# Six rescales per pass issued as two halves with a signal each, and a re-woven order of segments

## Chip, cores, metric

One Trainium2 chip, one core of it. The metric is device time in microseconds of one execution; lower is better. The whole program, from the first load to the last store, is one launch.

## What is computed

`x` is (64, 64, 128) float32: 64 sequences of 64 tokens with 128 features. Twelve layers follow each other, each on a layer norm of `x` and added to it:

```python
x = x + _L0_xattn_ref(ctx_1024, _layernorm(x), ...)   # 16 heads of attention over context and latents
x = x + _L0_attn_ref(_layernorm(x), ...)              # gated recurrence over the 64 tokens
x = x + _L0_ffn_ref(_layernorm(x), ...)               # 8 LoRA experts, top 2 of 10
x = x + _L1_xattn_ref(_layernorm(x), ctx_1024, ...)   # one-head cross attention
x = x + _L1_attn_ref(_layernorm(x), ...)              # causal linear attention
x = x + _L1_ffn_ref(_layernorm(x), ...)               # a block of its own: attention, then 4 gated experts
x = x + _L2_xattn_ref(ctx_1024, _layernorm(x), ...)   # 8 heads over context and latents
x = x + _L2_attn_ref(_layernorm(x), ...)              # local attention
x = x + _L2_ffn_ref(_layernorm(x), ...)               # 8 experts, top 1 with capacity
x = x + _L3_xattn_ref(_layernorm(x), ctx_1024, ...)   # x W1 plus the mean of the context times W2
x = x + _L3_attn_ref(_layernorm(x), ...)              # convolution and a small state-space scan
x = x + _L3_ffn_ref(_layernorm(x), ...)               # 8 experts, top 1
```

## The kernel before

The 64 sequences go through in 4 passes (`PASSES`) of two *slots*, each slot 8 sequences, which is 512 tokens: four tiles of 128 tokens on the partitions, so a slot's `x` is 128x512 in SBUF. Each slot has its own buffers (`X`, `Z`, `P`, `T`, `big`, `small`, four PSUM banks) and walks through all twelve layers; the two slots share the engines, so that one computes while the other waits.

**Order.** For every engine the program of a slot is a Python generator that yields between *segments*: a segment is a wait or two and the few instructions behind it. `weave(program, ORDER[engine])` steps the two generators by a written-out row of bits, one bit for a segment: 0 takes the next segment of slot 0, 1 that of slot 1. Within a slot the order of segments is fixed; the bits alone say how the two slots are shuffled on that engine. Engines run their instructions strictly in this order: a segment that has to wait holds up whatever is behind it, of the other slot too.

**A norm.** DVE makes the moments of the four tiles (`moments`, L1360 and L1365) and the variance (L1380, signal `var`); POOL takes it to the power -1/2 (`inverse_root`, L1855, signal `rstd`); DVE multiplies the slot's 128x512 by it (`rescale`, L1375, signal `tok`); PE transposes the four tiles into PSUM (`turn`, L457, signal `zT_ps`); ACT copies them out to `Z` (L1089, signal `zT`); then PE starts the layer's matmuls. Where the layer's weights are centred beforehand, the mean isn't subtracted, and `rescale` reads `x` straight from `X`. Six norms of a pass are such, are turned by PE as four tiles, and are touched by the change: `rnn` (the recurrence), `x1` (L1 cross attention), `lin` (linear attention), `loc` (local attention), `ssm`, `m3` (the last experts). The rescales of the others (`m1`, `rms`, `x2`, `x0`, `ctx0`, `ctx1`) stay whole. Six norms in four passes of two slots make 48 rescales.

**Around it.** In the attention over context and latents (`heads`) PE makes scores (L485), DVE their maxima (L1392), ACT the exponentials (L1114), DVE the reciprocal of the sums (L1400), POOL the normalisation (L1882), PE the transposes (L496), the mixing (L576 to L584) and the output projection (`out_of`, L504, 8 matmuls to a tile). The gated experts (`moe1`) run L815 and L825 on PE, L1679 on DVE, L1972 on POOL, L472 on PE. The experts of `moe2` and `moe3` run L868 and L872 (up), L1287 on ACT, L472 (down) on PE. For the first `heads` of the next pass POOL multiplies and shifts the context tokens, 128x1024 each (`affine`, L1892 and L1896); in POOL's program of a slot these two stand right behind the inverse root of `m3`.

```python
def inverse_root(s, i, name, n=4):
    yield
    pool.wait_ge(*on("var", s, i, name))
    pool.tensor_tensor(rstd(s, name, n), variance(s, name, n), mhalf[:, 0:n], ALU.pow)...
...
yield from inverse_root(s, i, "m3")
if i < PASSES - 1:
    yield from kv_context(s, i)
```

## Time and profile before

| | |
|---|---|
| median of 3 runs | 2494.84 us (2493.54 to 2503.49) |
| profiled execution, its own time | 2495.97 us |
| its span in the trace | 2494.2 us |
| PE busy | 2345.5 us, 94% |
| DVE, ACT, POOL busy | 1481.6, 1178.3, 930.0 us |
| granted TensorE clock, mean | 0.988 |

A row of a timeline gives the start and the length in us, the engine, the line, the operation, output<-inputs by name (slot numbers left out), the shape, the count, and in brackets how long the engine had sat idle before it and what ended that. On PE a float32 matmul is two records (a row with x16 is 8 of them); a transpose is one. PEld is PE's weight load, which runs beside PE.

### The profile page before, as it was taken

The page shows a single profiled execution, that of the slowest core. Times are in us where ns is not written, and L with a number is a line of the kernel's source. Part 1 is how long each engine was busy: PE and PEld are TensorE (multiplying, and loading weights), DVE is VectorE, ACT ScalarE, POOL GpSimd, SP SyncE. Part 2 cuts the span into 40 slices and gives each one's busy share as a digit, 9 for nine tenths or more (in the row PEclk, how much of TensorE's full clock was granted, in tenths as well). Part 3 has the DMA queues.
Part 4 walks back from the last instruction along what each step waited for, and adds up shares of the span by engine and source line. Part 5 has one row for each costly group of instructions (what it writes and reads, how often), then busy time and mean ns, then how long its engine had stood idle before and what let it go on. Part 6 is the DMA issues. An engine that isn't in the chain of part 4 may idle for free.

```text
span 2494.2 us, 41897 instructions
## 1 busy us (share of the span) xinstructions
PE 2345.5 (94%) x16412; PEld 1563.5 (63%) x16412; DVE 1481.6 (59%) x4040; ACT 1178.3 (47%) x2994; POOL 930.0 (37%) x853
## 2 busy tenths in 40 slices
PE   8999999999999999999999999999999999999998
PEld 5666665656756665666666665566566666656665
DVE  5457566665575667666564567665555555664653
ACT  4554334455444534545554444445454444354543
POOL 5334253533233335434231344443332242544310
PEclk8999999999999999999999999999999999999999
DMA  5000000000000000000000000000000000000000
GB/s 233 1 1 2 1 9 8 11 1 18 1 1 10 1 1 10 9 10 9 10 1 9 1 1 9 1 10 9 14 1 1 5 1 1 1 1 1 2 1 9
DMA packets 6677, 26.57 MB, mean 11 GB/s; under 512 B 848, under 2 KB 848, under 8 KB 5840
## 3 DMA queue, kind: packets, MB, share of 16 engines
q1 hardware_dynamic: 6480, 23.89, 2.6%
q8 instruction: 130, 2.13, 0.3%
q14 instruction: 67, 0.55, 0.1%
HBM read 21.79 MB, written 2.10 MB: 10 GB/s over the span
## 4 chain that ended last, share of the span: by engine, by line
PE 72%; DVE 17%; POOL 4%; ACT 4%; issue 3%; DMA 0%; SPq 0%; DVEq 0%; POOLq 0%; ACTq 0%
PE ps L472 10%; PE ps L485 7%; PE ps L529 6%; PE ps L504 6%; PE ps L868 4%; PE ps L496 3%; PE ps L608 3%; PE ps L457 3%; PE ps L583 3%; PE ps L576 3%; PE ps L630 3%; PE ps L581 2%; PE ps L825 2%; PE ps L815 2%; PE ps L657 2%
## 5 line engine op out<-in xcount | busy, mean ns | idle before, releaser
L1882 POOL TENSOR_TENSOR P<-P,small 128x384 f32<-128x384 f32 x384 | 317.2, 849 | 550.1 <-DVE small L1400 549.8
L1114 ACT ACTIVATE P<-ps,small 128x192 f32<-128x192 f32 x768 | 313.6, 420 | 155.1 <-DVE small L1392 153.5
L1855 POOL TENSOR_TENSOR small<-small,mhalf 128x4 f32<-128x4 f32 x112 | 129.0, 1152 | 547.2 <-DVE small L1380 315.4
L485 PE MATMUL ps<-kvT,big 128*128 128x192 f32 x1536 | 314.1, 335 | 6.7 <-DVE big L1407 2.5
L485 PEld LDWEIGHTS ps<-kvT,big 128*128 128x128 f32 x1536 | 248.6, 191 | 89.7 <-issue 52.8
L1392 DVE TENSOR_REDUCE small<-ps 128x2 f32<-128x384 f32 x384 | 210.1, 551 | 107.5 <-PE ps L485 100.2
L472 PEld LDWEIGHTS ps<-wts,P 128*128 128x128 f32 x1920 | 231.5, 192 | 43.8 <-issue 30.0
L472 PE MATMUL ps<-wts,P 128*128 128x128 f32 x1920 | 249.0, 279 | 5.2 <-POOL P L1972 2.6
L1972 POOL TENSOR_TENSOR P<-T 128x512 f32<-128x512 f32 x96 | 126.6, 1319 | 206.6 <-ACT T L1261 107.7
L504 PEld LDWEIGHTS ps<-value,big 128*128 128x128 f32 x1536 | 177.8, 192 | 25.8 <-issue 19.6
L504 PE MATMUL ps<-value,big 128*128 128x128 f32 x1536 | 188.0, 277 | 0.0
L529 PE MATMUL ps<-kvT,score 128*128 128x512 f32 x384 | 179.5, 609 | 5.9 <-ACT kvT L1089 4.7
L496 PE MATMUL ps<-cst,P 128*128 128x128 f32 x1152 | 166.5, 278 | 18.6 <-POOL P L1882 9.2
L496 PEld LDWEIGHTS ps<-cst,P 128*128 128x128 f32 x1152 | 132.5, 143 | 50.4 <-issue 18.6
L1114 ACT ACTIVATION_READ_ACCUMULATOR P<-ps,small 128x1 f32 x768 | 156.8, 204 | 0.0
L1287 ACT ACTIVATE P<-ps,col 128x512 f32<-128x512 f32 x128 | 81.2, 683 | 132.9 <-PE ps L872 132.8
L372 POOL TENSOR_TENSOR big<-big,cst 128x1024 f32<-128x1024 f32 x48 | 106.6, 2222 | 68.9 <-ACT big L1279 39.3
L1458 DVE SCALAR_TENSOR_TENSOR X<-ps,small,X 128x128 f32<-128x128 f32 x256 | 71.9, 343 | 98.9 <-PE ps L472 93.4
L608 PEld LDWEIGHTS ps<-Vbd,P 128*64 128x64 f32 x3072 | 98.2, 138 | 48.3 <-issue 34.7
L1597 DVE TENSOR_REDUCE small<-ps 128x8 f32<-128x512 f32 x128 | 87.7, 685 | 59.7 <-PE ps L630 59.5
L529 PEld LDWEIGHTS ps<-kvT,score 128*128 128x128 f32 x384 | 69.8, 193 | 83.5 <-issue 73.7
L1131 ACT ACTIVATE big<-ps 128x512 f32<-128x512 f32 x96 | 57.2, 596 | 132.5 <-PE ps L496 132.2
(281 smaller groups left out, 4476.8 us busy)
## 6 DMA issues: line engine op xcount, KB each, us to landing
ctok<-ctok_dram SPq DMA_DIRECT2D x8, 512.0 KB, 3.5
ctxT<-ctx_dram SPq DMA_DIRECT2D x8, 512.0 KB, 3.5
wts<-weights_dram SPq DMA_DIRECT2D x1, 2530.0 KB, 23.9
wts<-weights_dram SPq DMA_DIRECT2D x1, 2189.0 KB, 18.3
X<-x_dram SPq DMA_DIRECT2D x8, 256.0 KB, 3.0
big<-fold_dram SPq DMA_DIRECT2D x2, 1024.0 KB, 9.2
out_dram<-X SPq DMA_DIRECT2D x8, 256.0 KB, 2.0
wts<-weights_dram SPq DMA_DIRECT2D x1, 1536.0 KB, 27.0
```

Source lines behind the costliest of these rows:

```text
L372: return engine.tensor_tensor(big[s][:, 1024 * (t % 2):1024 * (t % 2) + 1024].rearrange("p (b j t) -> p b j t", b=2, t=SEQ), src[:, 128 * ...
L472: m = pe.matmul(part(s, k, t), tile_of(src, t), w, start=first and t == 0 and c == 0, stop=last and t == TILES - 1 and c == len(pairs) - 1)
L485: m = pe.matmul(ps[s][:, at:at + KEYS], big[s][:, BANK * b + 128 * p:BANK * b + 128 * p + 128], kvT[s][:, keys_at(b):keys_at(b) + KEYS], s ...
L496: m = pe.transpose(part(s, k, p), probs(s, j)[:, PAIR * p + at:PAIR * p + at + 128], C("ident"))
L504: m = pe.matmul(part(s, 1, t), big[s][:, 1024 * t + 128 * k:1024 * t + 128 * k + 128], value[:, at:at + 128], start=(t == 0 and k == 0), s ...
L529: m = pe.matmul(bank(s, qp_bank(g, r) + k), score[:, 128 * block_of(h, nh):128 * block_of(h, nh) + 128], latents(s), start=True, stop=True)
L608: m = pe.matmul(ps[s][64 * bb:64 * bb + 64, at:at + 18], src(bb, j), Vbd[s][:, 18 * (8 * b + j):18 * (8 * b + j) + 18], start=True, stop=True)
L1114: m = act.activation(probs(s, b // 2)[:, to:to + KEYS], ps[s][:, at:at + KEYS], ACT.Exp, bias=small[s][:, 4 * e + p:4 * e + p + 1], accum_ ...
L1392: dve.tensor_reduce(small[s][:, at:at + 2], ps[s][:, BANK * k:BANK * k + 2 * KEYS].rearrange("p (c k) -> p c k", k=KEYS), AX.X, ALU.max, n ...
L1855: pool.tensor_tensor(rstd(s, name, n), variance(s, name, n), mhalf[:, 0:n], ALU.pow).then_inc(*sig("rstd", s))
L1882: m = pool.tensor_tensor(view, view, over(small[s][:, at:at + 2], 2, [128, 2, KEYS]), ALU.mult)
L1972: pool.tensor_tensor(P[s][:, 1024 + 512 * (k % 2):1536 + 512 * (k % 2)], tmp(s, k % 2), tmp(s, 2 + k % 2), ALU.mult)\
```

## The change

`rescale_halves` issues the multiplication as two instructions of 128x256, tiles 0 and 1 and then tiles 2 and 3, each with its own signal on `tok`. `turn_halves` waits for the first signal before the transposes of tiles 0 and 1, and for the second before those of tiles 2 and 3; both waits lie in one segment, with no yield between them. The counts of `tok` are lengthened to fit. The bits of four engines are rewritten (each has as many as before, SP's are unchanged); one line of each table stands here.

```diff
 ORDER = dict(
     pe=(2496, int(""
-        "4120180e82000011000000000033dbffdf375f56bac10c1af4ddee629cc55cb06914148810afbdc018a1ca1dd3aea84c3e9c"
+        "20120316012000010800000200013bbfffe375f56bac8860cf4edeec616c55cb039141144409fba01e8a1c61ba9db58463e9"
...
+HALVED = ["rnn", "x1", "lin", "loc", "ssm", "m3"]
...
-MANY = {"kv": KV, "var": VARS, "rstd": VARS, "tok": TOKENS, ...
+MANY = {"kv": KV, "var": VARS, "rstd": VARS, "tok": halves(TOKENS), ...
...
+                def turn_halves(s, i, name, k, src):
+                    for t in range(TILES):
+                        if t % 2 == 0:
+                            pe.wait_ge(*on("tok", s, i, name if t else name + ".0"))
+                        m = pe.transpose(part(s, k, t), tile_of(src, t), C("ident"))
+                    m.then_inc(*sig("zT_ps", s))
...
-                    pe.wait_ge(*on("tok", s, i, "rnn"))
-                    turn(s, 0, N[s])
+                    turn_halves(s, i, "rnn", 0, N[s])          # likewise x1, lin, loc, ssm, m3
...
+                def rescale_halves(s, i, name, dst, src):
+                    yield
+                    dve.wait_ge(*on("rstd", s, i, name))
+                    for h in range(2):
+                        dve.tensor_tensor(by_tile(dst)[:, 2 * h:2 * h + 2, :], by_tile(src)[:, 2 * h:2 * h + 2, :],
+                                          over(rstd(s, name)[:, 2 * h:2 * h + 2], 2, [128, 2, D]), ALU.mult).then_inc(*sig("tok", s))
...
-                        yield from rescale(s, i, name, dst, src)
+                        yield from rescale_halves(s, i, name, dst, src)
```

In the changed kernel the lines have other numbers: L457 is L464 (and L471 where halved), L472 is L486, L485 is L499, L496 is L510, L504 is L518, L576 is L590, L868 and L872 are L878 and L882, L1375 is L1389 where halved, L1855 is L1870, L1882 is L1897, L1892 and L1896 are L1907 and L1911.

Between the two orders 776 of PE's 2229 segments that issue anything stand behind another number of the other slot's segments than before, most of them by one; they lie in 214 places, between which the orders agree.

**Place A, `m3` of slot 1 in the third pass.** PE before (`ps_1`, `P_1` are slot 1's; the L457 is the turn of `m3`, the L504 rows are `out_of` of slot 0):

```order
L583 MATMUL ps_0<-Z_0,T_0 128x512
L584 MATMUL ps_0<-Z_0,T_0 128x512
L504 MATMUL ps_0<-value0,big_0 128x128 x8
L457 MATMUL ps_1<-cst,P_1 128x128 x4
L504 MATMUL ps_0<-value0,big_0 128x128 x8
L683 MATMUL ps_0<-ctxT_0,wts 128x512 x2
```

The same place of PE now:

```order
L597 MATMUL ps_0<-Z_0,T_0 128x512
L598 MATMUL ps_0<-Z_0,T_0 128x512
L518 MATMUL ps_0<-value0,big_0 128x128 x16
L471 MATMUL ps_1<-cst,P_1 128x128 x4
L697 MATMUL ps_0<-ctxT_0,wts 128x512 x2
```

The turn has moved behind the last 8 matmuls of slot 0's `out_of`. POOL at the same place, before (`small_1` is slot 1's inverse root of `m3`, `T_1<-ctok_1` and `T_1<-T_1` are `affine` on its context):

```order
L1882 TENSOR_TENSOR P_0<-P_0,small_0 128x2x192 x16
L1855 TENSOR_TENSOR small_1<-small_1,mhalf 128x4
L1892 TENSOR_TENSOR T_1<-ctok_1,col 128x1024
L1896 TENSOR_TENSOR T_1<-T_1,col 128x1024
L1855 TENSOR_TENSOR small_0<-small_0,mhalf 128x4
```

and now:

```order
L1897 TENSOR_TENSOR P_0<-P_0,small_0 128x2x192 x16
L1870 TENSOR_TENSOR small_1<-small_1,mhalf 128x4
L1870 TENSOR_TENSOR small_0<-small_0,mhalf 128x4
L1907 TENSOR_TENSOR T_1<-ctok_1,col 128x1024
L1911 TENSOR_TENSOR T_1<-T_1,col 128x1024
```

Slot 0's inverse root, that of the next recurrence, now stands between slot 1's inverse root of `m3` and the two long operations on the context.

**Place B, PE in the third pass, slot 1 in `moe2` (L472, L868, L872), slot 0 in its first `heads` (L485, L496).** Before:

```order
L472 MATMUL ps_1<-wts,P_1 128x128 x8
L868 MATMUL ps_1<-A_1,wts 128x512 x2
L872 MATMUL ps_1<-mTb_1,pick_b 128x512 x2
L472 MATMUL ps_1<-wts,P_1 128x128 x8
L868 MATMUL ps_1<-A_1,wts 128x512 x2
L872 MATMUL ps_1<-mTb_1,pick_b 128x512 x2
L472 MATMUL ps_1<-wts,P_1 128x128 x16
L496 MATMUL ps_0<-cst,P_0 128x128 x4
L485 MATMUL ps_0<-kvT_0,big_0 128x192 x2
L496 MATMUL ps_0<-cst,P_0 128x128 x8
```

Now:

```order
L486 MATMUL ps_1<-wts,P_1 128x128 x4
L510 MATMUL ps_0<-cst,P_0 128x128 x4
L499 MATMUL ps_0<-kvT_0,big_0 128x192 x2
L486 MATMUL ps_1<-wts,P_1 128x128 x4
L878 MATMUL ps_1<-A_1,wts 128x512 x2
L882 MATMUL ps_1<-mTb_1,pick_b 128x512 x2
L486 MATMUL ps_1<-wts,P_1 128x128 x4
L510 MATMUL ps_0<-cst,P_0 128x128 x4
L486 MATMUL ps_1<-wts,P_1 128x128 x4
L510 MATMUL ps_0<-cst,P_0 128x128 x4
L878 MATMUL ps_1<-A_1,wts 128x512 x2
L882 MATMUL ps_1<-mTb_1,pick_b 128x512 x2
```

Slot 0's transposes and scores, which stood behind the experts of slot 1, are now spread between them.

**Place C, PE at the end of `moe1` of slot 1 in the last pass.** Before (the L472 x8 are the last two of twelve steps of the gated experts, L457 on `ctok_1` the turn of the context, `ps_0` is `heads` of slot 0):

```order
L825 MATMUL ps_1<-A_1,wts 128x512
L472 MATMUL ps_1<-wts,P_1 128x128 x8
L457 MATMUL ps_1<-cst,ctok_1 128x128 x8
L496 MATMUL ps_0<-cst,P_0 128x128 x4
L504 MATMUL ps_0<-value2,big_0 128x128 x8
L576 MATMUL ps_0<-big_0,T_0 128x512
```

Now:

```order
L836 MATMUL ps_1<-A_1,wts 128x512
L518 MATMUL ps_0<-value2,big_0 128x128 x8
L486 MATMUL ps_1<-wts,P_1 128x128 x8
L464 MATMUL ps_1<-cst,ctok_1 128x128 x8
L590 MATMUL ps_0<-big_0,T_0 128x512
```

Slot 0's 8 matmuls of `out_of` have moved ahead of the last two steps of slot 1's experts, and its four transposes further up.

## Rows read from the trace of the kernel before

**Rows 1.** The profile's page: span, busy time by engine, and the chain by engine.

```profile
span 2494.2 us, 41897 instructions
...
PE 2345.5 (94%) x16412; PEld 1563.5 (63%) x16412; DVE 1481.6 (59%) x4040; ACT 1178.3 (47%) x2994; POOL 930.0 (37%) x853
...
PE 72%; DVE 17%; POOL 4%; ACT 4%; issue 3%; DMA 0%; SPq 0%; DVEq 0%; POOLq 0%; ACTq 0%
```

**Rows 2.** PE's waits by releaser: us in total, times, longest.

```profile
PE ps L457 <- DVE P L1375: 33.0, 42, 2.9
PE ps L496 <- POOL P L1882: 9.2, 14, 2.2
```

**Rows 3.** Timeline, `x1` of slot 1, first pass: first of 25 halved turns that waited.

```profile
310.04 1.02 POOL L1855 TENSOR_TENSOR small<-small,mhalf 128x4 f32<-128x4 f32 x1
...
311.10 0.69 DVE L1375 TENSOR_TENSOR P<-X,small 128x512 f32<-128x512 f32 x1 [0.55 <-POOL small L1855]
...
311.85 0.66 PE L457 MATMUL ps<-cst,P 128*128 128x128 f32 x4 [0.42 <-DVE P L1375]
```

**Rows 4.** Timeline, `m3` of slot 0, last pass: the last of the 25.

```profile
2445.02 0.65 PE L457 MATMUL ps<-cst,P 128*128 128x128 f32 x4 [1.80 <-DVE P L1375]
```

**Rows 5.** DVE groups by form: count, then busy us and mean ns of one.

```profile
L1598 DVE TENSOR_TENSOR P<-ps,small 128x512 f32<-128x512 f32 x128 | 88.5, 691 | 4.4
...
L1360 DVE BATCH_NORM_STATS2 small<-X 128x6 f32<-128x128 f32 x384 | 83.3, 279 | 6.1 <-DMA X<-x_dram 4.0
...
L1587 DVE TENSOR_TENSOR kvT<-ps,small 128x128 f32<-128x128 f32 x96 | 28.0, 291 | 3.3
```

**Rows 6.** PE's transposes at L457: duration in ns, min/median/max.

```profile
L457 PE MATMUL ps<-cst,P x352: 272/273/477, 11.8 to 2464.8; 128*128 128x128 f32 x176
```

**Rows 7.** Rescales at L1375 fed from `X`: duration in ns, min/median/max.

```profile
L1375 DVE TENSOR_TENSOR P<-X,small x48: 679/692/2480, 131.1 to 2462.8; 128x512 f32<-128x512 f32 x48
```

**Rows 8.** Timeline, `lin` of slot 1, first pass: first of 14 long rescales.

```profile
330.38 1.27 POOL L1972 TENSOR_TENSOR P<-T 128x512 f32<-128x512 f32 x1
330.44 1.75 DVE L1375 TENSOR_TENSOR P<-X,small 128x512 f32<-128x512 f32 x1 [0.53 <-POOL small L1855]
331.72 2.33 POOL L1892 TENSOR_TENSOR T<-ctok,col 128x1024 f32<-128x1024 f32 x1
```

**Rows 9.** Timeline around place A, `m3` of slot 1, third pass: last of the 14.

```profile
1930.01 1.01 POOL L1855 TENSOR_TENSOR small<-small,mhalf 128x4 f32<-128x4 f32 x1 [8.13 <-DVE small L1380]
...
1930.39 2.05 PE L504 MATMUL ps<-value,big 128*128 128x128 f32 x16
...
1930.98 2.00 POOL L1892 TENSOR_TENSOR T<-ctok,col 128x1024 f32<-128x1024 f32 x1
1931.05 2.48 DVE L1375 TENSOR_TENSOR P<-X,small 128x512 f32<-128x512 f32 x1 [1.12 <-POOL small L1855]
1933.06 2.32 POOL L1896 TENSOR_TENSOR T<-T,col 128x1024 f32<-128x1024 f32 x1
1933.45 0.68 DVE L1432 COPY big<-ps 128x512 f32<-128x512 f32 x1
...
1933.58 0.66 PE L457 MATMUL ps<-cst,P 128*128 128x128 f32 x4 [1.15 <-DVE P L1375]
```

**Rows 10.** Timeline, two scans back to back on DVE, POOL beside them.

```profile
286.85 2.08 POOL L1972 TENSOR_TENSOR P<-T 128x512 f32<-128x512 f32 x1 [1.48 <-ACT T L1261]
...
288.43 3.71 DVE L1472 TENSOR_TENSOR_SCAN big<-T,big 128x512 f32<-128x512 f32 x2
...
289.45 1.61 POOL L1972 TENSOR_TENSOR P<-T 128x512 f32<-128x512 f32 x1 [0.53 <-ACT T L1261]
```

**Rows 11.** The scans at L1472: duration in ns, min/median/max.

```profile
L1472 DVE TENSOR_TENSOR_SCAN big<-T,big x16: 1190/1225/2215, 149.4 to 2115.2; 128x512 f32<-128x512 f32 x16
```

**Rows 12.** POOL groups by form: count, then busy us and mean ns of one.

```profile
L1882 POOL TENSOR_TENSOR P<-P,small 128x384 f32<-128x384 f32 x384 | 317.2, 849 | 550.1 <-DVE small L1400 549.8
```

**Rows 13.** Timeline: the first of 46 waits whose segments now stand further back.

```profile
22.92 2.41 PE L529 MATMUL ps<-kvT,score 128*128 128x512 f32 x5 [1.10 <-ACT kvT L1089]
```

**Rows 14.** Timeline around place C: the last of the 46.

```profile
2276.20 1.26 POOL L1972 TENSOR_TENSOR P<-T 128x512 f32<-128x512 f32 x1 [1.01 <-ACT T L1261]
...
2277.52 1.16 PE L472 MATMUL ps<-wts,P 128*128 128x128 f32 x8 [1.11 <-POOL P L1972]
```

**Rows 15.** Timeline around place B.

```profile
1233.17 2.06 POOL L1882 TENSOR_TENSOR P<-P,small 128x384 f32<-128x384 f32 x2
...
1246.28 0.87 DVE L1458 SCALAR_TENSOR_TENSOR X<-ps,small,X 128x128 f32<-128x128 f32 x3 [11.73 <-PE ps L472]
```

More of the change, by code:

```diff
@@ new lines @@
+        "d930588ed73eb000018bfb2ffcecffd1dc40001008c56b483bc0930120ffd181f870101383a86d33fd6febfbbc28717efb7e"
+        "9acfc54b5bfff6dbee707114148a04fdef5401c918e6c09d54163eb74d30b4c5ae72000038bfb75ff1affb4f44482672eb78"
+        "8286dcfb7fc181102c86940200004c21bfcff936fd6ebffffb785c77075f56ee5928a5d76703911029140503ef3e901c24c9"
+        "9baea857fff7779f27120aad5400007d5dfd4f15d1b4010069bbbc330a01525fbfff1942d00e20800000056bfd97eef375f5"
+        "ff83141ae9bffefeef8ff28cef6b8ca502245053c5eee80b111167de3481cff7fffffb87ffbbdfffff9e292cd1eeb2a22410"
@@ new lines @@
+        "2bec7ff19e1d404e9fffc0f", 16)),
+    act=(1740, int(""
+        "40402207000020008000335fff93f6f4fbbfa7548613430f00901c00083079ecbe87de270440ed9d6218fee366fff6840049"
+        "0de383bc09469e1801a0079e0ccfbdfedbfffde96e60cf3ff5dd4b1b00902c2020cace60ef07de3ca18433b100f2fecb0fff"
+        "f5870cdfaf8823b1dc00c8f9a0010000f4f393fdeffffb3fefedf3102c5aa28f00841048208195db4f63fff73d38401eb489"
+        "8f8ff885f9100d73f7a610113ab768f9c00000009db9e7dbf3fbfbbfffcf9b60b955d12c10416040801eb3bf501fbffffddf"
+        "fcfffff246863cefd2492b1c2ffa00fff1", 16)),
@@ L97 @@
         "67fd", 16)),
     pool=(610, int(""
-        "673400df30532b53182161b93a2fbb7378c7904c253ac34fc0ff53185609d43957dee378c7cb219c0e0dee3a2b53142131b5"
-        "3af57f8db607c0b9807706bc935fa660ac0ae49ffff3be7d1d", 16)),
+        "ca028adf3036335290a1c27a3937bdc9fd2c90489531671fc0ff66225518e8392fbe71f9b58d059a0d0ef635335490a07279"
+        "3cf5df371d23c0b9805c56f4a3cfaa612a0ccc9fffdfe67d1d", 16)),
     sp=(26, int(""
@@ L133, with halves @@
 PROJ = ["rnn.g", "rnn.i", "lin", "lin.v", "m1", "m1.p1", "m1.v", "loc", "loc.v"]
-MANY = {"kv": KV, "var": VARS, "rstd": VARS, "tok": TOKENS, "zT_ps": TURNS, "zT": COPIES, "y_ps": SUMS, "x_biased": BIASED,
+HALVED = ["rnn", "x1", "lin", "loc", "ssm", "m3"]
+def halves(names):
+    return [m for n in names for m in ([n + ".0", n] if n in HALVED else [n])]
+MANY = {"kv": KV, "var": VARS, "rstd": VARS, "tok": halves(TOKENS), "zT_ps": TURNS, "zT": COPIES, "y_ps": SUMS, "x_biased": BIASED,
         "logits": LOGITS, "shifted": LOGITS[:3], "u_exp": LOGITS[:3], "n_proj": PROJ,
@@ L724, in cross @@
                     yield
-                    pe.wait_ge(*on("tok", s, i, "x1"))
-                    turn(s, 0, N[s])
+                    turn_halves(s, i, "x1", 0, N[s])
                     yield
@@ L751, in linear @@
                     yield
-                    pe.wait_ge(*on("tok", s, i, "lin"))
-                    turn(s, 0, N[s])
+                    turn_halves(s, i, "lin", 0, N[s])
                     yield
@@ L847, in local @@
                     yield
-                    pe.wait_ge(*on("tok", s, i, "loc"))
-                    turn(s, 0, N[s])
+                    turn_halves(s, i, "loc", 0, N[s])
                     yield
@@ L947, in ssm @@
                     yield
-                    pe.wait_ge(*on("tok", s, i, "ssm"))
-                    turn(s, 0, N[s])
+                    turn_halves(s, i, "ssm", 0, N[s])
                     for ks in ((0,), (1,), (2, 3)):
@@ L974, in moe3 @@
                     yield
-                    pe.wait_ge(*on("tok", s, i, "m3"))
-                    turn(s, 0, N[s])
+                    turn_halves(s, i, "m3", 0, N[s])
                     yield
@@ L1701, in local @@
                        .then_inc(*sig("x3_sum", s))
-                    yield from rescale(s, i, "loc", N[s], res(s, i))
+                    yield from rescale_halves(s, i, "loc", N[s], res(s, i))
                     yield
```

21 lines of the change are left out of this document (5 added, 16 removed).

## The prediction, made before the changed kernel had run

> **What bounds the kernel now.** I read the page first: PE is busy for 2345.5 of 2494.2 us, no other engine for over 59%, and PE makes 72% of the chain that ended last [rows 1]. So PE is idle for 2494.2 - 2345.5 = 148.7 us in all, and nothing that leaves PE's work as it is can bring more than that; the change takes no matmul away. What the change can move is these 148.7 us. The waits of PE by releaser say what they are made of: the largest group is the turn behind a rescale, 33.0 us in 42 waits, the next is the transposes of `heads` behind POOL, 9.2 us [rows 2]; the rest is spread over some forty small groups. Then I went to the timeline of the six norms. Of their 48 turns 25 waited, the first for 0.42 us [rows 3] and the last for 1.80 us [rows 4], 18.8 us together. The others found their rescale done.
>
> **Part 1, the halves.** An undisturbed rescale takes 0.69 us, and PE's transposes start 0.06 us behind its end (311.10 + 0.69 = 311.79, then 311.85 [rows 3]). The trace has no DVE operation of 128x256 of this kind. A product of 128x128 takes 291 ns and one of 128x512 takes 691 ns [rows 5], so each further column costs 400/384 = 1.04 ns, and 256 columns come to 291 + 133 = 424 ns. Two operations with no wait between them overlap a little: the 384 moments have a mean of 279 ns but cover 83.3 us, 217 ns each [rows 5], so the next starts 62 ns before the end of the last. The second half then starts at 362 ns and ends at 786 ns. The first signal comes 268 ns earlier than now, the last 94 ns later.
>
> On PE four transposes take 0.66 us [rows 3] and one 273 ns [rows 6], so they are 0.13 us apart. Behind the first signal (0.42 + 0.06 = 0.48 us) two transposes issue until 0.74; the second signal is there at 0.79 + 0.06 = 0.85; the last two end at 0.85 + 0.13 + 0.27 = 1.25 us. Now they end at 0.69 + 0.06 + 0.66 = 1.41 us. That is 0.16 us for each turn that waits, 25 x 0.16 = 4 us. The bounds: 25 x 0.27 = 6.7 us, if the second pair were never late, and below nothing the 94 ns that each of 48 rescales adds on DVE, 4.5 us, if DVE were always what PE waits for. DVE is busy for 59% [rows 1] and mostly waits itself, so I take 4 us gained and 0 lost.
>
> **Part 2, POOL and the shared access of a rescale.** The rescales of the six norms lie between 679 and 2480 ns, with a median of 692 [rows 7]; 14 of the 48 took over 0.9 us, the first at 330.44 [rows 8] and the last at 1931.05 [rows 9]. Each long one starts while POOL runs a large operation and ends some 0.5 us after it: POOL's L1892 runs from 1930.98 to 1932.98, the rescale from 1931.05 to 1933.53, and POOL's next, L1896, takes 2.32 us instead of 2.00 [rows 9]. So DVE and POOL hold each other up, a whole instruction at a time. Two scans back to back show what happens between two DVE instructions: each takes 1190 ns alone [rows 11], the pair took 3.71 us, and a POOL operation that came up during the first one (289.45) was through before the second ended [rows 10]. POOL gets in between.
>
> That bears on the halves: where a POOL operation is waiting when the first half ends, the second half waits for all of it. In the order before, the six `m3` of the first three passes have L1892 ahead of the rescale and L1896 right behind, and the second half would wait 2.0 us there [rows 9]. The Trainium skill says the same from the other side (SBUF — State Buffer, section "Who interferes with whom"): a Vector instruction with two inputs in SBUF contends with a GpSimd instruction that reads SBUF, and the one that starts first holds the access for the whole instruction. By it each half asks anew; it speaks against this change wherever POOL has work queued, and the traced scans agree with it.
>
> But POOL's order is changed just there. Place A shows it: the other slot's inverse root now stands between the root of `m3` and L1892. In three of the six (slot 0 in the first and third pass, slot 1 in the third) something stands there now, and in the other three work of the other slot (two or four normalisations, or short operations and an inverse root) stands between L1892 and L1896, so that the long L1896 is not waiting when the first half ends. Where L1892 is late, the rescale is free of it and ends up to 2.48 - 0.69 = 1.8 us earlier; PE waited 1.15 us for it at place A [rows 9] and like times at the other two. Bounds: 0 (normalisations of 849 ns each [rows 12] take the place of L1892) to 3 x 1.15 = 3.5 us; I take 2 us. Against it, second halves that meet a normalisation elsewhere: I take 2 of the 14 at 0.85 us, 2 us. The part comes to 0.
>
> **Part 3, the order.** PE changes in 214 places, half of them exchanges of two neighbouring segments. I went through PE's waits of over 0.1 us and looked at where their segments now stand. 46 of them, 30.0 us in all, have more of the other slot's work ahead than before, the first at 22.92 [rows 13] and the last at 2277.52 [rows 14]; by the length of that work 24.3 us of them could be filled. 13 waits, 6.0 us, have less ahead. At place C PE waited 1.11 us for POOL's L1972 [rows 14], and now does 8 matmuls of `out_of` there, 2.05 us a set of the same size [rows 9]; that wait is filled whole. At place A the moved `out_of` needs the copy L1432, which DVE makes behind the rescale, from 1933.45 to 1934.13 [rows 9]: with the old rescale it would not be ready in time, and the move pays only because POOL's order frees the rescale as well. So of two places looked at, one pays by itself and one by its companion. Place B is of another kind: up to 1246.28 DVE had nothing to do for 11.73 us while PE ran the experts of slot 1, although POOL had slot 0's probabilities ready at 1235.23 [rows 15]. Now slot 0's transposes stand between the experts; PE gains nothing there at once, but slot 0's chain of DVE, ACT and POOL gets some microseconds of lead, and the experts that are left cover its later waits.
>
> A segment put forward into a place where its input isn't ready opens a new wait, and the trace of before can't show these; every one of the filled waits also makes its own slot later. The bounds are 24.3 us gained, and 0. I take half, 12 us, as one of the two places pays alone.
>
> **The sum.** 4 + 0 + 12 = 16 us against the profiled execution's own 2495.97 us gives 2480 us; that execution was 1.1 us over the median of the runs, so against 2494.84 the prediction is 2479 us, 0.6% less. About 0.5%, 12.5 us, is what a measurement of this kernel can tell from no change, so the forecast lies just outside of it, at 2482.4.
>
> **The rivals.**
>
> - *The waits only move* (22%). Both slots' chains are as long as before; a filled wait comes back one segment later, since what was put ahead delays the slot that waits. For it: most waits are under 1 us and spread over the whole span, which is how a well-woven order looks. Against it: 46 waits get cover and 13 lose it. Then part 3 gives 0 and the halves 4 us: 2491 us.
> - *The experts as a reserve pay more* (8%). As at place B, more of the latency of `heads` is hidden than the single waits say. Nearly all of the 24.3 us, the 4 and the 3.5: 2463 us.
> - *POOL takes the gap between the halves* (12%), the one that ends slower. Place: the second half of the 14 rescales that met POOL before. Price: 2.0 us at the 6 of `m3` and at the 2 of `lin` with L1892 behind [rows 8], 0.85 us [rows 12] at the other 6, 8 x 2.0 + 6 x 0.85 = 21 us on DVE, and PE waits within a segment, so nothing can pass. It decides if POOL's order brings its readers there as often as before and the order's fills come to less than 21 - 4 - 12.5 = 4.5 us; with none of them it gives 2494.8 + 21 - 4 = 2512 us. The skill's rule named above is this rival's rule. Against it: place A's new POOL order.
> - The forecast holds the remaining 58%, with a range of its own from 2470 to 2487 us.
>
> **The numbers.** The range reaches from 24.3 + 6.7 + 3.5 us below the median, 2460, to the halves' cost on DVE of 4.5 us with no fill, 2499 us. It leaves out nearly all of the slower rival and a part of the third case, under 2 in 10. Faster by over 0.5%: four fifths of the forecast and all of the large case, 0.55. Within 0.5%: the rest of the forecast and the first rival, 0.33. Slower: 0.12.
>
> **What would show it.** The 48 rescales appear as 96 operations of 128x256 with a median near 424 ns; PE's waits behind them in total fall from 18.8 us to about 14 or less. The rescales of `m3` beside L1907 are fewer than five at over 2 us. PE's busy time stays at 2345 us within a few us and its idle time falls to about 133 us. DVE's longest idle near place B is shorter than 11.73 us. I would be wrong if second halves last over 1 us at many places (then POOL is in the gap), if PE's waits by releaser keep their total under other names (then the waits only moved), or if PE's busy time changes by more than 5 us, since then the interleaving itself costs something that I put at nothing.

## The result: 2526.34 us, 1.2% slower than before

The changed kernel took 2526.34 us (median of 4, 2523.93 to 2528.49), beside 2494.79 us of the kernel before: ratio 1.0116, 95% interval 1.0094 to 1.0139. I had predicted 2479 us and a range up to 2499; the time lies 31.5 us over the kernel before and outside of the range. The page of the changed kernel (span, busy time by engine, chain by engine), to be read beside [rows 1]:

```profile
span 2526.4 us, 41947 instructions
...
PE 2362.1 (93%) x16412; PEld 1573.7 (62%) x16412; DVE 1494.2 (59%) x4088; ACT 1165.8 (46%) x2994; POOL 918.4 (36%) x853
...
PE 68%; DVE 18%; ACT 5%; POOL 4%; issue 4%; DMA 0%; SPq 0%; DVEq 0%; POOLq 0%; ACTq 0%
```

The span grew by 32.2 us. PE's busy time grew by 2362.1 - 2345.5 = 16.6 us with the same 16412 matmuls, and its idle time from 148.7 to 2526.4 - 2362.1 = 164.3 us. The chain is now 68% PE instead of 72%. PE's waits by releaser (us in total, times, longest):

```profile
PE ps L471 <- DVE P L1389: 18.9, 23, 1.7
PE ps L510 <- POOL P L1897: 12.4, 19, 2.3
PE ps L464 <- DVE P L1383: 9.4, 13, 2.8
```

The turns that were halved (L471) waited 18.9 us, as much as the same 48 turns did before (18.8 us). The transposes of `heads` behind POOL grew from 9.2 [rows 2] to 12.4 us. The halves are the new group on DVE (duration in ns, min/median/max):

```profile
L1389 DVE TENSOR_TENSOR P<-X,small x96: 394/421/2222, 133.9 to 2495.3; 128x256 f32<-128x256 f32 x96
```

**Place A** after the change, timeline:

```profile
1952.84 1.01 POOL L1870 TENSOR_TENSOR small<-small,mhalf 128x4 f32<-128x4 f32 x1 [3.53 <-DVE small L1395]
1953.88 0.76 DVE L1389 TENSOR_TENSOR P<-X,small 128x256 f32<-128x256 f32 x2 [1.12 <-POOL small L1870]
...
1959.71 0.60 PE L471 MATMUL ps<-cst,P 128*128 128x128 f32 x4
...
1962.21 1.01 POOL L1870 TENSOR_TENSOR small<-small,mhalf 128x4 f32<-128x4 f32 x1 [8.36 <-DVE small L1395]
1963.18 2.00 POOL L1907 TENSOR_TENSOR T<-ctok,col 128x1024 f32<-128x1024 f32 x1
1963.25 4.35 DVE L1389 TENSOR_TENSOR P<-X,small 128x256 f32<-128x256 f32 x2 [1.12 <-POOL small L1870]
1965.26 2.06 POOL L1911 TENSOR_TENSOR T<-T,col 128x1024 f32<-128x1024 f32 x1
1965.51 0.44 PE L471 MATMUL ps<-cst,P 128*128 128x128 f32 x2 [0.87 <-DVE P L1389]
1967.65 0.44 PE L471 MATMUL ps<-cst,P 128*128 128x128 f32 x2 [1.70 <-DVE P L1389]
```

The rescale of `m3` of slot 1 is free, as forecast: two halves in 0.76 us, and its turn found them ready (the wait of 1.15 us of [rows 9] is gone). But what POOL's order put ahead of L1907 is slot 0's inverse root, and behind an inverse root comes a rescale. The two long operations now meet the halves of slot 0's recurrence: 4.35 us, and PE waits 0.87 and 1.70 us. The meeting moved by one norm. Nor are the other `m3` all free: the six pairs of halves of the first three passes take 1.36, 2.96, 2.55, 1.69, 2.01 and 0.76 us in order of time. And two meetings stand as they stood, at `lin` of slot 1 in the first and the third pass (3.63 and 3.62 us), which are those of [rows 8] in halves:

```profile
334.54 3.63 DVE L1389 TENSOR_TENSOR P<-X,small 128x256 f32<-128x256 f32 x2 [0.54 <-POOL small L1870]
335.82 2.06 POOL L1907 TENSOR_TENSOR T<-ctok,col 128x1024 f32<-128x1024 f32 x1
...
338.22 0.69 PE L471 MATMUL ps<-cst,P 128*128 128x128 f32 x2 [1.71 <-DVE P L1389]
```

**Place C** is filled as forecast; slot 0's 16 records of `out_of` run where PE had waited 1.11 us [rows 14], and no row has a wait:

```profile
2305.59 1.02 PE L836 MATMUL ps<-A,wts 128*128 128x512 f32 x2
2306.45 1.95 PE L518 MATMUL ps<-value,big 128*128 128x128 f32 x16
...
2308.24 1.95 PE L486 MATMUL ps<-wts,P 128*128 128x128 f32 x16
```

### The profile page after: what moved, and what is told of

Read it like the earlier page. It is cut to its first block, busy times and chain, and to the rows that moved or that the text cites. A ratio compares the mean times of both kernels' runs of the same rounds, so it can differ in the third digit from the quotient of the medians.

```text
span 2526.4 us, 41947 instructions
## 1 busy us (share of the span) xinstructions
PE 2362.1 (93%) x16412; PEld 1573.7 (62%) x16412; DVE 1494.2 (59%) x4088; ACT 1165.8 (46%) x2994; POOL 918.4 (36%) x853
## 4 chain that ended last, share of the span: by engine, by line
PE 68%; DVE 18%; ACT 5%; POOL 4%; issue 4%; DMA 0%; SPq 0%; DVEq 0%; POOLq 0%; ACTq 0%
PE ps L486 10%; PE ps L499 6%; PE ps L518 6%; PE ps L543 5%; PE ps L878 4%; PE ps L510 3%; PE ps L622 3%; PE ps L597 3%; PE ps L590 2%; PE ps L644 2%; PE ps L595 2%; PE ps L836 2%; PE ps L826 2%; PE ps L464 2%; PE ps L671 2%
## 5 line engine op out<-in xcount | busy, mean ns | idle before, releaser
L1897 POOL TENSOR_TENSOR P<-P,small 128x384 f32<-128x384 f32 x384 | 318.2, 851 | 551.8 <-DVE small L1415 551.7
L1122 ACT ACTIVATE P<-ps,small 128x192 f32<-128x192 f32 x768 | 314.1, 422 | 148.7 <-DVE small L1407 148.1
L1870 POOL TENSOR_TENSOR small<-small,mhalf 128x4 f32<-128x4 f32 x112 | 127.2, 1136 | 594.2 <-DVE small L1395 318.1
L499 PE MATMUL ps<-kvT,big 128*128 128x192 f32 x1536 | 316.3, 335 | 9.6 <-ACT P L1122 3.5
L499 PEld LDWEIGHTS ps<-kvT,big 128*128 128x128 f32 x1536 | 248.2, 191 | 95.8 <-issue 55.1
L486 PEld LDWEIGHTS ps<-wts,P 128*128 128x128 f32 x1920 | 234.9, 195 | 52.7 <-issue 35.1
L486 PE MATMUL ps<-wts,P 128*128 128x128 f32 x1920 | 254.2, 282 | 8.9 <-DVE P L1808 4.4
L518 PEld LDWEIGHTS ps<-value,big 128*128 128x128 f32 x1536 | 178.2, 192 | 28.3 <-issue 18.4
L518 PE MATMUL ps<-value,big 128*128 128x128 f32 x1536 | 188.9, 278 | 2.0 <-ACT P L1122 1.8
L510 PE MATMUL ps<-cst,P 128*128 128x128 f32 x1152 | 167.3, 278 | 20.1 <-POOL P L1897 12.4
L510 PEld LDWEIGHTS ps<-cst,P 128*128 128x128 f32 x1152 | 132.6, 142 | 50.3 <-issue 17.2
L1269 ACT ACTIVATE T<-ps 128x512 f32<-128x512 f32 x96 | 57.3, 596 | 120.4 <-PE ps L836 120.3
```

What stands on the lines that cost most here:

```text
L486: m = pe.matmul(part(s, k, t), tile_of(src, t), w, start=first and t == 0 and c == 0, stop=last and t == TILES - 1 and c == len(pairs) - 1)
L499: m = pe.matmul(ps[s][:, at:at + KEYS], big[s][:, BANK * b + 128 * p:BANK * b + 128 * p + 128], kvT[s][:, keys_at(b):keys_at(b) + KEYS], s ...
L510: m = pe.transpose(part(s, k, p), probs(s, j)[:, PAIR * p + at:PAIR * p + at + 128], C("ident"))
L518: m = pe.matmul(part(s, 1, t), big[s][:, 1024 * t + 128 * k:1024 * t + 128 * k + 128], value[:, at:at + 128], start=(t == 0 and k == 0), s ...
L1122: m = act.activation(probs(s, b // 2)[:, to:to + KEYS], ps[s][:, at:at + KEYS], ACT.Exp, bias=small[s][:, 4 * e + p:4 * e + p + 1], accum_ ...
L1897: m = pool.tensor_tensor(view, view, over(small[s][:, at:at + 2], 2, [128, 2, KEYS]), ALU.mult)
```

## The experiments

Every ratio is to the kernel before, run beside the version on the same chip; its median there was between 2495.28 and 2500.61 us, so I compare ratios, not medians. Its single executions differ with the granted clock, as 2491.06 us at a mean of 0.992 and 2502.57 us at 0.985 beside e1 to e4. "Old order" means the four tables of the kernel before.

| run | median us | ratio | 95% interval |
|---|---|---|---|
| e1 halves, old order | 2512.17 | 1.0053 | 1.0033, 1.0073 |
| e2 whole rescales, new order | 2519.19 | 1.0087 | 1.0062, 1.0112 |
| e3 halves, one wait, old order | 2518.90 | 1.0081 | 1.0055, 1.0107 |
| e4 `rnn` and `loc` halved, old order | 2494.68 | 0.9984 | 0.9971, 0.9997 |
| e5 whole, PE's table new | 2573.77 | 1.0322 | 1.0302, 1.0342 |
| e6 whole, the other tables new | 2607.00 | 1.0449 | 1.0431, 1.0466 |
| e7 halves, old order, POOL waits | 2491.44 | 0.9985 | 0.9968, 1.0003 |
| e8 whole, old order, POOL waits | 2494.33 | 0.9988 | 0.9973, 1.0004 |
| e9 whole, new order, quiet stretches | 2494.69 | 0.9996 | 0.9986, 1.0005 |
| e10 whole, new order, the others | 2522.01 | 1.0102 | 1.0084, 1.0120 |
| e11 the changed kernel, POOL waits | 2531.03 | 1.0147 | 1.0127, 1.0166 |
| e12 e7 and a second wait of POOL | 2494.74 | 0.9994 | 0.9985, 1.0002 |
| e13 whole, new order 510 to 945 us | 2512.00 | 1.0052 | 1.0034, 1.0070 |
| e14 whole, new order 1480 to 2165 us | 2508.58 | 1.0034 | 1.0022, 1.0046 |
| e15 whole, 100 exchanges on PE | 2535.15 | 1.0150 | 1.0133, 1.0167 |
| e16 whole, 54 exchanges on DVE | 2536.49 | 1.0140 | 1.0118, 1.0162 |
| e17 whole, 37 exchanges that delay no one | 2499.63 | 1.0007 | 0.9994, 1.0020 |
| e18 e7 with these 37 | 2492.55 | 0.9981 | 0.9972, 0.9991 |

### Each part alone: e1 to e4

e1 keeps the halves and takes the old order; e2 the reverse; e3 and e4 vary e1.

```diff
 ORDER = dict(
     pe=(2496, int(""
-        "20120316012000010800000200013bbfffe375f56bac8860cf4edeec616c55cb039141144409fba01e8a1c61ba9db58463e9"
+        "4120180e82000011000000000033dbffdf375f56bac10c1af4ddee629cc55cb06914148810afbdc018a1ca1dd3aea84c3e9c"
...
```

> The halves of all six norms, with the four order tables of the kernel before. Theory H (POOL gets between the halves and PE pays for it): the 21 us of the slower rival on DVE come back here, since the old order has POOL's readers right behind the long rescales; with the 4 us that PE gains, about 2494.8 + 17 = 2510 us, and second halves of over 2 us at most of the six m3. Theory O (the order tables are what costs): the halves alone give 2490 to 2497 us, and nearly all of the 31 us lie in the order.

e2, with whole rescales and one wait (`HALVED = []`) under the new tables:

> The changed order tables with whole rescales and one wait per turn. Theory H: without halves the new order costs little, 2490 to 2505 us. Theory O: 2520 us or more, near the changed kernel's 2526. If the two parts add up, this and the halves on the old order together make +31 us.

e3:

```diff
-                        if t % 2 == 0:
-                            pe.wait_ge(*on("tok", s, i, name if t else name + ".0"))
+                        if t == 0:
+                            pe.wait_ge(*on("tok", s, i, name))
```

> Halves on DVE as in the change, old order, but PE waits only for the second signal of each turn before all four transposes. What DVE and POOL do is the same as with the halves on the old order; only PE's early start is taken away. The prediction's step of 0.16 us for each of 25 waiting turns makes this 4 us slower than the halves on the old order; if a turn whose second half is late gained nothing from its first, they are the same within 2 us.

e4:

```diff
-HALVED = ["rnn", "x1", "lin", "loc", "ssm", "m3"]
+HALVED = ["rnn", "loc"]
```

> Halves only for rnn and loc on the old order, the two norms whose 16 rescales never met a reading operation of POOL at their start in the trace before (one of loc had one that began in the middle of it). Theory H: no second half is late, so 7 waiting turns gain 0.16 us each: 2492 to 2495 us, no loss. If halving costs by itself (an added instruction and signal on DVE), it is slower than before by more than 2 us here too.

Both parts lose, and they nearly add up: 0.53% + 0.87% = 1.40% beside 1.16%. The halves cost 13 us in the old order (e1); the new order costs 22 us with no half in it (e2). Without PE's early start the halves cost 0.81%, 20 us (e3), so the early start is worth 0.28%, 7 us. The two norms that rarely meet POOL lose nothing when halved: 0.9984, with an interval that ends below 1 (e4). e1's trace at `m3` of slot 0 in the third pass:

```profile
1770.48 2.00 POOL L1907 TENSOR_TENSOR T<-ctok,col 128x1024 f32<-128x1024 f32 x1
1770.54 4.35 DVE L1389 TENSOR_TENSOR P<-X,small 128x256 f32<-128x256 f32 x2 [0.53 <-POOL small L1870]
...
1772.56 2.06 POOL L1911 TENSOR_TENSOR T<-T,col 128x1024 f32<-128x1024 f32 x1
...
1772.81 0.44 PE L471 MATMUL ps<-cst,P 128*128 128x128 f32 x2 [1.30 <-DVE P L1389]
...
1774.95 0.44 PE L471 MATMUL ps<-cst,P 128*128 128x128 f32 x2 [1.70 <-DVE P L1389]
```

DVE and POOL take turns, one instruction each: POOL's L1907, the first half behind it, L1911 in the gap, the second half behind that. Whole, such a rescale took 2.48 us and PE waited once [rows 9]; in halves it takes 4.35 us and PE waits twice. And there is a second price. The same trace by stretches (length, PE, PEld, DVE, ACT and POOL busy, then PEclk, DMA share, GB/s), the stall and what follows it:

```profile
1768.00:1775.50 7.50, 4.50 (x32) 3.27 (x32) 6.30 (x12) 1.27 (x3) 5.42 (x4) 1.00 0.00 0
1776.00:1782.00 6.00, 5.92 (x16) 3.41 (x16) 3.88 (x25) 0.02 (x1) 1.02 (x1) 0.50 0.01 3
```

Behind a stretch in which PE was idle for 3.0 of 7.5 us, its clock was granted at 0.50, the level of 1.2 GHz, and PE's next rows are long:

```profile
1776.08 1.88 PE L492 MATMUL ps<-wts,Z 128*128 128x8 f32 x8 [0.25 <-ACT Z L1097]
1777.81 3.76 PE L878 MATMUL ps<-Z,wts 128*128 128x512 f32 x4
```

At the level of 2.4 GHz the same two take 1.06 and 1.96 us (e7, below). From the trace of before to that of e1, PE's idle time rises only from 148.7 to 152.1 us, and its busy time by 10.7 us. About 5 us of the 10.7 are the clock, an estimate from the mean clocks of the two profiled executions (0.988 and 0.986, over 2500 us). The ratio 1.0053 isn't made of it: the executions of the kernel before beside e1 had 0.986 in the median, as those of e1.

### Only one side of the new order: e5, e6

On PE, 203 of the 214 changed places take the new table in e5 and the other engines keep theirs; e6 is the reverse (457 of 485 places of DVE, ACT and POOL). The places left out are those at which the engines would wait for each other in a circle. From here on a cut about tables says how they were made; the kernels hold the numbers that came out.

```diff
-    pe=NEW, act=NEW, dve=NEW, pool=NEW
+    pe=NEW, act=OLD, dve=OLD, pool=OLD      # e5; e6: pe=OLD, the others NEW
```

> Whole rescales; PE's table takes 203 of its 214 changed places from the new order (the other 11 would deadlock alone), while DVE, ACT and POOL keep the old one. Theory P (PE's exchanges put segments in front whose input is late, and PE waits there): most of the 22 us that the new order cost come back, about 2510 us or more. Theory D (the order of DVE, ACT and POOL makes the results that PE waits for later, and PE's own exchanges only fill waits): about 2485 to 2495 us.

> Whole rescales; PE keeps the old table, DVE, ACT and POOL take 457 of their 485 changed places from the new order. Theory D: about 2510 us or more. Theory P: about 2490 to 2500 us. If the tables only fit each other as a set, both this and the PE table alone are slower than the new order as a whole, 2519 us.

3.2% and 4.5%, both far worse than the whole set's 0.9%. The tables only fit each other; this says nothing on which engine's table is the bad one.

### POOL kept out of the gap: e7, e8, e12, e11

```diff
                         pool.wait_ge(*on("ssm_g", s, i))
+                        pool.wait_ge(*on("tok", s, i, "m3"))
```

POOL's two long operations on the context may start only when both halves of `m3` are done. e7 has it with halves, e8 with whole rescales.

> All halves on the old order, with one wait added on POOL: the multiplication of the context tokens waits for the second half of the m3 rescale, so that it can't run ahead of it or between the halves. Theory H (POOL in the gap at m3 makes the loss of the halves, 13 us): the six long second halves of m3 are gone, and with them most of the loss; 2493 to 2500 us. If the loss of the halves has another cause, it stays at about 2508 to 2512 us.

> Whole rescales on the old order with the same wait on POOL. It takes away the collision that makes six m3 rescales last 1.8 to 2.5 us before the change too: DVE gets 6 times 1.8 us back, PE waited 1.1 to 1.6 us at four of them, so 5 us faster than before, 2488 us, if POOL's delay of 0.8 us is hidden; no change if the waits only move.

The loss of the halves is gone: 1.0053 became 0.9985. The same `m3` in e7, the same two rows of PE behind it, and the stretch around them:

```profile
1763.42 0.76 DVE L1389 TENSOR_TENSOR P<-X,small 128x256 f32<-128x256 f32 x2 [0.53 <-POOL small L1870]
...
1764.22 0.60 PE L471 MATMUL ps<-cst,P 128*128 128x128 f32 x4
1764.31 2.00 POOL L1907 TENSOR_TENSOR T<-ctok,col 128x1024 f32<-128x1024 f32 x1 [0.93 <-issue]
...
1764.66 0.60 PE L510 MATMUL ps<-cst,P 128*128 128x128 f32 x4
...
1765.56 1.06 PE L492 MATMUL ps<-wts,Z 128*128 128x8 f32 x8 [0.30 <-ACT Z L1097]
1766.47 1.96 PE L878 MATMUL ps<-Z,wts 128*128 128x512 f32 x4
```

```profile
1765.60:1771.60 6.00, 5.95 (x38) 4.34 (x39) 4.18 (x26) 2.23 (x4) 4.09 (x3) 1.00 0.01 3
```

0.76 us instead of 4.35, no wait of PE at the turn, and the clock stays at its level of 2.4 GHz. POOL's later start costs nothing that can be measured (e8); nor does it bring the 5 us that I expected of it where the rescales are whole. Halves beside whole, both with this wait, are 0.9985 beside 0.9988: the halves by themselves bring at most what a measurement can't tell from nothing.

e12 adds a second wait, for `lin` of slot 1, where POOL's operation on the context of the second `heads` stood in the gap:

```diff
                         pool.wait_ge(*on("m1_g", s, i, MOE1_K - 1))
+                        if s == 0:
+                            pool.wait_ge(*on("tok", 1, i, "lin"))
                         yield from affine(s, i, "x2.ctx", ...)
```

> Old order, halves, POOL waits for m3's tokens before its operations on the context as in the earlier run, and also slot 0's operation on the context of the second heads waits for slot 1's linear norm. Two second halves of 2.21 us (332.09 and 1551.86 in the earlier run) should fall to about 0.4 us, with PE's waits of 1.70 and 1.05 us behind them. Theory H: 2 to 3 us less than the earlier run's 2491.4, so ratio to before 0.997 to 0.998. Rival, POOL's late start delays the heads behind it by as much: ratio 0.9985 as there.

Not the 2 to 3 us more that I expected: 0.9994 beside 0.9985, intervals overlapping. In the trace the two meetings are gone (the longest half takes 1.49 us instead of 2.22, PE's waits behind halves sum to 10.3 us instead of 13.0), but the time isn't shorter. And e11 puts e7's wait into the changed kernel:

> The changed kernel, with POOL's operations on the context made to wait for both halves of m3. In the changed kernel's profile one second half of m3 still waits for L1911 (1965.38, PE idle for 1.70 us behind it) and three first halves overlap L1907. Theory H, halves cost only where POOL stands in the gap, and the new order's own loss stays: halves in the new order cost about 7 us (2526 against 2519), and this wait takes back 2 to 5 us of them, so 2521 to 2524 us against the 2526 of the changed kernel, ratio to before near 1.009 to 1.011. If the order's loss came from the same meeting of POOL and DVE at m3, the time would fall to below 2510 us, ratio under 1.005.

It took nothing back (1.0147 beside 1.0116). At place A the trace says why: `m3` is free already, and the meeting is with the recurrence, for which this wait does nothing; the expectation had taken the wait of 1.70 us there for one behind `m3`. At the two `m3` of 2.96 and 2.55 us the wait did end the meeting, and the time shows nothing of it. The recurrence in e11:

```profile
1963.43 2.00 POOL L1907 TENSOR_TENSOR T<-ctok,col 128x1024 f32<-128x1024 f32 x1
1963.49 4.35 DVE L1389 TENSOR_TENSOR P<-X,small 128x256 f32<-128x256 f32 x2 [1.12 <-POOL small L1870]
```

### Where the order loses: e2's trace, e9, e10, e13, e14

In e2's trace I looked up each of PE's segments and compared its wait with that of the same segment before. Segments that stand behind more of the other slot's work than before: 30.3 us of waits became 7.0. Those that stand behind less: 6.3 became 21.4. Those that stand where they stood: 103.3 became 125.2. So 23.3 us were filled, as the prediction had it (24.3), and 37.0 us of waits grew elsewhere. Place A in e2, where nothing is halved:

```profile
1944.13 0.69 DVE L1387 TENSOR_TENSOR P<-X,small 128x512 f32<-128x512 f32 x1 [1.12 <-POOL small L1877]
...
1953.44 2.00 POOL L1914 TENSOR_TENSOR T<-ctok,col 128x1024 f32<-128x1024 f32 x1
1953.50 2.48 DVE L1387 TENSOR_TENSOR P<-X,small 128x512 f32<-128x512 f32 x1 [1.12 <-POOL small L1877]
...
1956.04 0.66 PE L464 MATMUL ps<-cst,P 128*128 128x128 f32 x4 [1.15 <-DVE P L1387]
...
1957.94 0.60 PE L482 MATMUL ps<-cst,small 128*8 128x128 f32 x4 [1.25 <-DVE small L1539]
```

The 1.15 us that were filled at the turn of `m3` stand now at the turn of slot 0's recurrence, six us behind that of `m3`, and DVE, held up there for 2.48 us, makes the one-hot rows of slot 1's last experts (L1539) late as well: 1.25 us more. One wait was filled and two came.

The lateness of e2 against before, read at the same segments, grew in two stretches (510 to 945 us and 1480 to 2165 us) and from 2210 us on, and not in the others. Since the tables agree between the changed places, they can be spliced:

```diff
+for a, b in windows:                     # e9: 0-510, 945-1480, 2165-2210; e10: the rest
+    for e in ("pe", "act", "dve", "pool"):
+        tab[e][cut(e, a):cut(e, b)] = new[e][cut(e, a):cut(e, b)]      # tab begins as the old table
```

> Whole rescales. The new order stands only in the three stretches in which the execution with the whole new order lost nothing against the old one (0 to 510, 945 to 1480 and 2165 to 2210 us), the old order elsewhere; 94 of the 214 changed places of PE are in it. In the profile of the whole new order these stretches together gained 6.1 us. Theory P, the loss belongs to places and each keeps its effect without the others: about 6 us below the kernel before, ratio near 0.9976. Theory S, the loss is spread over the exchanges whatever the stretch and depends on what earlier ones handed on: 94/214 of 20.6 us, 9 us above, ratio near 1.0036.

> Whole rescales. The complement: the new order in 510 to 945, 1480 to 2165 and from 2210 us on, the old one elsewhere; 120 of PE's 214 changed places. In the profile of the whole new order these stretches lost 26.6 us. Theory P: 26 us above the kernel before, ratio near 1.0106. Theory S: 120/214 of 20.6 us, 11.5 us above, ratio near 1.0046.

> Whole rescales, the new order only from 510 to 945 us, the old one elsewhere (38 of PE's 214 changed places). The kernel with the new order in all three losing stretches was 1.0102 of the kernel before, and its lateness grew by 11.5 to 14 us in this stretch. Theory P, the loss belongs to places: 11 to 14 us, ratio 1.0045 to 1.0055. Rival, the loss needs the other stretches too (a handed-on state): ratio under 1.002.

> Whole rescales, the new order only from 1480 to 2165 us (58 of PE's 214 changed places). Theory P: what is left of 1.0102, 11 to 13 us, ratio 1.0045 to 1.0055, and with the stretch from 510 to 945 it sums to the 25 us of the three. Rival: ratio under 1.002.

Each stretch loses by itself: 0.52% and 0.34% make most of the 1.02% of e10, and the quiet stretches cost nothing (0.9996), though the gain of 6 us that e2's trace promised for them isn't there either. So the loss sits at places and is not handed on; but it is at many of them, since no step of e10's lateness is over 2.5 us. What sets the stretches apart is what was filled, not what was opened: by e2's trace 14.3 us of waits were filled and 18.4 us opened in the quiet ones, 9.0 us filled and 18.0 us opened in the others.

### What one exchange costs: e15 to e18

Old order, whole rescales, and two neighbouring segments exchanged where by the trace of before the segment put forward had been ready for over 0.3 us and the other didn't wait: on PE 100 drawn at random from 309 such pairs, on DVE all 54. No wait can open for the segment put forward.

```diff
+l[k], l[k + 1] = l[k + 1], l[k]          # 100 such k on PE (e15), 54 on DVE (e16)
```

> Whole rescales, the old order of all other engines; on PE 100 exchanges of two neighbouring segments of the two slots, drawn at random from the 309 pairs in which, by the trace of before, the segment put forward had its inputs over 0.3 us earlier (median 2.7 us) and the other did not wait. No exchange can open a wait for the segment put forward or fill one; each makes the other segment's results later by the length of its neighbour, 1.06 us in the median. Theory D, an exchange costs by what it delays, and the order before was already near its best: some 0.1 us each, as the whole new order's 20.6 us over 214 places, so 5 to 20 us, ratio 1.002 to 1.008, with the growth in PE's idle time at segments that did not move. Rival N, delays of a microsecond vanish in the engines' slack and only exchanges that open a wait cost: ratio 0.999 to 1.001.

> The same on DVE alone: 54 exchanges, all pairs in which the segment put forward had its inputs over 0.3 us earlier (median 2.3 us) and the other did not wait; PE, ACT and POOL keep the old order. DVE is busy for 59% only, PE for 94%. Theory D: each delays a result by 1.2 us that PE may be waiting for, 0.1 us each, 5 us, ratio near 1.002. Rival N: ratio 0.999 to 1.001.

1.0150 and 1.0140: 37 us for 100 exchanges on PE, 0.37 us each, and 35 us for 54 on DVE, 0.65 us each. On DVE a good part of the price is the clock: four of e16's five executions have a mean of 0.980 (the fifth, at 0.986, took 2525.22 us), the kernel before beside them 0.986 in the median and e15 0.987. Over 2500 us a step of 0.006 is 15 us, an estimate, and leaves 20 us, 0.37 us each. Theory D had the direction; it expected 1.002 to 1.008 of e15 and 1.002 of e16, so its size was too small. In e15 none of the 200 exchanged segments waits in either trace; the waits of the other 2029 grew from 139.9 to 169.7 us. One of the 100, before and in e15, where slot 0's projection (L472, in e15 L469) has been put behind four matmuls of slot 1 (L529, in e15 L526; 1.88 us):

```profile
1693.33 1.05 PE L472 MATMUL ps<-wts,kvT 128*128 128x128 f32 x8
...
1694.49 0.69 DVE L1449 TENSOR_TENSOR X<-ps,X 128x512 f32<-128x512 f32 x1 [0.20 <-PE ps L472]
1695.22 0.87 DVE L1360 BATCH_NORM_STATS2 small<-X 128x6 f32<-128x128 f32 x4
1695.94 0.60 PE L457 MATMUL ps<-cst,X 128*128 128x128 f32 x4
```

```profile
1721.05 1.05 PE L469 MATMUL ps<-wts,kvT 128*128 128x128 f32 x8
...
1722.21 0.69 DVE L1450 TENSOR_TENSOR X<-ps,X 128x512 f32<-128x512 f32 x1 [1.91 <-PE ps L469]
1722.93 0.87 DVE L1351 BATCH_NORM_STATS2 small<-X 128x6 f32<-128x128 f32 x4
1723.28 0.66 PE L443 MATMUL ps<-cst,X 128*128 128x128 f32 x4 [1.18 <-DVE small L1351]
```

Before, DVE waited 0.20 us for L472, and the 1.88 us of slot 1's matmuls behind it covered DVE's addition and the moments, so the turn (L457) had no wait. With these matmuls ahead, DVE waits 1.91 us, the cover is used up, and the turn waits 1.18 us.

In 76 of the 100 the segment put back was awaited: another segment starts within 0.3 us of its end. The change's own 94 exchanges of two neighbours on PE are of the same make: in 73 of them the segment put back was awaited so, by 85 us of delay in sum. The control, only exchanges in which nobody waits for the segment put back:

```diff
+if slack(y) > 0.3 and awaited(x) > length(y) + 0.5:     # all 22 such k on PE, all 15 on DVE
+    l[k], l[k + 1] = l[k + 1], l[k]
```

> Whole rescales, the old order but for 37 exchanges of two neighbouring segments (22 on PE, 15 on DVE), all those in which by the trace of before the segment put forward had its inputs over 0.3 us earlier and the segment put back is first waited for at least 0.5 us later than the exchange can make it late, or by no one. Of the 100 random exchanges on PE only 7 were of this kind, of the 54 on DVE 15. Theory D, an exchange costs by the delay of what another engine waits for: these cost nothing, and as most segments put forward on PE are taken at once by a waiting engine, some of it may come back as a gain: ratio 0.996 to 1.001. Rival T, a touched place costs as such (0.35 us on PE, 0.65 us on DVE, as the random ones did): 22 x 0.35 + 15 x 0.65 = 17 us, ratio near 1.007.

> The version that the runs point to: old order with the same 37 exchanges, the rescales as halves, and POOL's operations on the context waiting for both halves of m3. The halves with this wait had 0.9985 of the kernel before. Theory D: the exchanges keep their effect, so 0.9985 times that of the run above, 0.995 to 1.000. Rival T: near 1.005.

1.0007 (0.9994 to 1.0020) where the price by touched place would have been 1.007. So it is the delay handed to an engine that waits which costs, not the exchange. Nor is there a gain in putting forward what is awaited. For the change's own tables this is argued from the 73 of 94 and from the waits that opened: no run has the new order with only the awaited segments left in their places. e18, halves and POOL's wait with these exchanges, has the lowest ratio, 0.9981 (0.9972 to 0.9991), 4.7 us and far under the 0.5% that I had set for telling a change; beside e4 (0.9984) it is the only version whose interval lies below 1, and beside e7 (0.9985) it isn't told apart. It beats the changed kernel by 1.3%.

## Why the prediction was wrong, step by step

The sum was 4 + 0 + 12 = 16 us gained. Measured, the halves lose about 7 us in the new order and the order loses 22 us, which makes 29 of the 31.5 us.

- **Part 1, the halves.** The form was right: 421 ns to a half (424 estimated), 0.76 us for an undisturbed pair (0.786). PE's early start is worth 7 us (e3 against e1) where I had 4, at the bound of 6.7: probably because it counts at the stretched rescales too, which I had left out. With POOL kept away, halves and whole differ by nothing measurable (e7, e8).
- **Part 2, put at 0, was the first step that failed.** In the old order the meeting costs 20 us, 13 behind PE's early start, and in the changed kernel the halves still cost 1.0116 - 1.0087 = 0.29%, 7 us, though here the two intervals overlap. I let POOL's new order pay for it: of the three `m3` that I counted as freed, the one at place A was freed and its partner, slot 0's recurrence, was caught instead; the other two take 1.36 and 2.01 us. The two `lin` of [rows 8] I priced in the rival and left out of this part; they take 3.6 us each. I had seen that slot 0's inverse root stands ahead of L1892, and had not asked which rescale follows that one. The Trainium skill's rule (SBUF — State Buffer, section "Who interferes with whom"), that the one which starts first holds the access for its whole instruction, is borne out by e1's rows: 4.35 us for two halves with POOL between them. I had the rule and the scans [rows 10] and gave their consequence 12%.
- **Part 3, 12 us gained, was the larger failure.** What was filled came out as worked out: 23.3 us of 24.3. The step that failed is the other bound, "The bounds are 24.3 us gained, and 0". I wrote that every filled wait makes its own slot later and then priced it at nothing worse than giving back the gain. Measured, 15.1 us of waits opened at segments put ahead and 21.9 us at segments that did not move at all, and the order alone costs 22 us (e2). I looked at PE's waits, which say where an order could be better, and not at what ran without a wait, which is where it can get worse: for 76 of the 100 segments that e15 put back, another started within 0.3 us of their end.
- **The rivals.** "POOL takes the gap" was right in its mechanism and nearly in its price: 21 us, or 17 behind the gain of PE, where the old order shows 20 (e3) and 13 (e1). In the new order it is 7, and the larger cause is another. "The waits only move" had the mechanism of the order and too kind a price, 0.
- **Marks.** The halves' median, the `m3` beside L1907 (three over 2 us, fewer than five) and the missing waits at places A and C came as said; DVE's longest wait behind the experts fell from 11.7 to 9.3 us, as place B had it. PE's waits behind the halves did not fall to 14 us (18.9), and its idle time is 164.3 us, not 133. Of the signs of being wrong two came: 11 of the 48 second halves last over 1 us, and PE's busy time rose by 16.6 us where I had set 5. What the 16.6 us are isn't settled. By the mean granted clock, 0.988 in both profiled executions, they aren't the clock; e2 and e15 have 7.3 and 8.5 us more busy time at 0.988 too. One piece can be read in e7's rows: four transposes take 0.60 us, and where nothing waits the next row begins 0.44 us after their start, so a wait opened behind them makes 0.16 us more busy time. How much that adds up to isn't known.

## What to carry to other kernels

Before an instruction is split, look at what the other user of its operands' access has queued: each gap between two parts lets one of its operations in, so either split where that engine has nothing to run, or make it wait. Judge a change of a static order not by the waits it fills but by the segments it puts back: a segment for whose result another engine stands idle should stay where it is, and an exchange of two neighbours that opens no wait for the one put forward cost 0.37 us on the busiest engine and 0.65 us, the clock's part included, on one that is busy for only 59%. When an exchange moves an operation past another, follow what comes behind that other one, too.

## What the hardware showed that I had not expected

- PE's clock can be a price on top of a stall: behind 3.0 us of idle time within 7.5 us it ran at 0.50 for the 6 us looked at, and four records of 128x512 took 3.76 us instead of 1.96. In e16 its mean fell from 0.986 to 0.980, about 15 of the 35 us lost (an estimate).
- Slack on an engine doesn't make delays there free: 54 exchanges on DVE, busy for 59%, cost nearly as much as 100 on PE, busy for 94%.
